# Graph layer on one core: score tables read back by source tile in rows of 2,000 bytes, each piece behind the wait for its own bucket

## What is computed

```python
e = xl[src] + xr[dst]
e = jnp.where(e >= 0, e, NEG_SLOPE * e)
score = jnp.einsum('ehd,hd->eh', e, att)          # 20,000 edges x 4 heads
m = jax.ops.segment_max(score, dst, num_segments=N)
ex = jnp.exp(score - m[dst])
denom = jax.ops.segment_sum(ex, dst, num_segments=N)
alpha = ex / (denom[dst] + SM_EPS)
agg = jax.ops.segment_sum(alpha[:, :, None] * xl[src], dst, num_segments=N)
```

## Time and profile before

| | |
|---|---|
| median of 3 runs | 1064.28 us (1063.62 to 1066.21) |
| profiled execution | 1064.61 us, span 1062.9 us |
| PE busy | 847.4 us (80%) |
| VectorE busy | 779.2 us (73%) |
| ScalarE busy | 352.6 us (33%) |
| POOL busy | 389.4 us (37%), of it the scatters L2314 240.3 us in 184 instructions |
| scatters, first and last start | 113.4 and 482.0 us |
| granted TensorE clock, mean | 0.887 |

### The profile page before, as it was taken

How to read it: one execution, slowest core, us unless ns; L and a number is a source line. 1 busy time by engine, 2 the same in 40 slices (tenths; PEclk the granted TensorE clock), 3 DMA queues, 4 the chain that set the end, 5 groups by cost and what they waited for, 6 DMA issues and landing times.

```text
span 1062.9 us, 18331 instructions
## 1 busy us (share of the span) xinstructions
PE 847.4 (80%) x5485; PEld 737.6 (69%) x5485; DVE 779.2 (73%) x2013; ACT 352.6 (33%) x1004; POOL 389.4 (37%) x321
## 2 busy tenths in 40 slices
PE   4898779895999896803389999758993895899997
PEld 2577667774788885803279999745892684788996
DVE  7778887888766689934778886776879657766636
ACT  0277443452664356602011111002550261221120
POOL 3279365776576656761032221500000000311204
PEclk9998879997999997866579999979896996799999
DMA  8750000002203234210179999730000001788883
GB/s 283 239 169 1 2 2 3 3 3 59 40 4 72 46 80 96 59 21 20 51 253 315 319 325 337 272 130 0 1 2 0 1 2 46 290 292 299 299 334 99
DMA packets 39511, 129.36 MB, mean 122 GB/s; under 512 B 13117, under 2 KB 22411, under 8 KB 31395
## 3 DMA queue, kind: packets, MB, share of 16 engines
q1 hardware_dynamic: 22974, 112.64, 32.0%
q0 software_dynamic: 10464, 8.67, 4.5%
q10 hardware_dynamic: 5992, 7.04, 1.9%
HBM read 108.83 MB, written 19.26 MB: 121 GB/s over the span
## 4 chain that ended last, share of the span: by engine, by line
PE 43%; DMA 18%; POOL 15%; DVE 14%; issue 9%; ACT 1%; POOLq 0%; SPq 0%; DVEq 0%; ACTq 0%
POOL pair_scores L2314 12%; PE bank L880 12%; DMA pair_scores<-arena,pair_cells 12%; PE bank L891 6%; PE bank L600 4%; PE bank L813 4%; DMA arena<-in_exp 2%; POOL arena L2348 2%; PE bank L802 2%; PE bank L668 2%; PE bank L978 2%; PE bank L534 2%; DMA arena<-slot_y,sloti 2%; PE bank L1025 1%; PE bank L524 1%
## 5 line engine op out<-in xcount | busy, mean ns | idle before, releaser
L2314 POOL DMA_INDIRECT pair_scores<-arena,pair_cells x184 | 240.3, 1306 | 137.6 <-DMA pair_scores<-arena,pair_cells 62.7
L2338 POOL DMA_INDIRECT arena<-row_tab,ids x42 | 57.7, 1375 | 440.4 <-DVE ids L1724 433.5
L880 PE MATMUL bank<-arena 128*128 128x128 f32 x1480 | 181.3, 281 | 2.4 <-DMA arena<-in_exp 2.3
L880 PEld LDWEIGHTS bank<-arena 128*128 128x128 f32 x1480 | 175.9, 198 | 4.2 <-DMA arena<-in_exp 3.2
L668 PE MATMUL bank<-x_hi,hot 125*125 x368 | 118.8, 348 | 6.8 <-issue 1.4
L2071 ACT ACTIVATE tc<-bank 125x256 f32<-125x256 f32 x184 | 70.5, 384 | 134.9 <-PE bank L668 126.4
L668 PE MATMUL bank<-x_lo,hot 125*125 x368 | 104.8, 305 | 0.0
L891 PE MATMUL bank<-arena 128*128 128x256 f32 (+1 forms) x404 | 97.5, 384 | 1.3 <-issue 1.3
L668 PEld LDWEIGHTS bank<-x_hi,hot 125*125 125x125 f32 x368 | 76.0, 207 | 20.7 <-issue 18.0
L1302 DVE TENSOR_TENSOR tc<-tc,vec 125x512 f32<-125x512 f32 x92 | 63.8, 693 | 33.9 <-ACT tc L2072 32.4
L802 PE MATMUL bank<-ident,arena 125*125 125x125 f32 x260 | 44.4, 306 | 50.9 <-ACT arena L2121 49.5
(11 more groups left out here) (410 smaller groups left out, 1691.2 us busy)
## 6 DMA issues: line engine op xcount, KB each, us to landing
arena<-in_exp SPq DMA_DIRECT2D x25, 1024.0 KB, 6.6
arena<-in_exp SPq DMA_DIRECT2D x17, 1386.0 KB, 6.2
arena<-in_exp0o SPq DMA_DIRECT2D x25, 512.0 KB, 6.5
pair_scores<-cnt SPq DMA_DIRECT2D x10, 1093.8 KB
arena<-in_exp1o SPq DMA_DIRECT2D x17, 640.0 KB
arena<-pair_scores SPq DMA_DIRECT2D x4, 1093.8 KB
slot_y<-arena ACTq DMA_DIRECT2D x34, 128.0 KB, 6.2
pair_scores<-arena,pair_cells POOLq DMA_INDIRECT x184
```

Source lines behind the costliest of these rows:

```text
L880: mm = pe.matmul(banks[1 + 2 * q + buf][0:rows, i * SLOTS:(i + 1) * SLOTS], w_in(s, q, k, m, rows), xsT[:, s, k, :], start=(k == 0), stop= ...
L2314: p.indirect_dma_start(out=pair_scores[which], in_=sc_ring[:, i, which, :], in_offset=None, out_offset=bass.IndirectOffsetOnAxis(ap=pair_c ...
L2338: p.indirect_dma_start(out=xs[:, q, :], out_offset=None, in_=tab, in_offset=bass.IndirectOffsetOnAxis(ap=ids[:, q, :], axis=0))\
```

## The change

`ENDS` becomes the 24 ends of buckets 0 to 23, so that each bucket but the last has its own. `load_table(m)` becomes a loop over the five source tiles: for each it awaits the scatters up to the end of bucket 5 m + s and loads the piece as tile 4's are loaded, four DMAs in rows of 2,000 bytes. The waits that stood ahead of whole tables go. VectorE's wait for a table counts the semaphores of 20 DMAs in place of 4. Tile 4's pieces are as before, with their ends under new indices; the order of tables, buffers, `h2` and `merged` is unchanged.

```diff
--- before.py
+++ after.py
@@ -80,7 +80,7 @@
 
 BASES = {"before": 0, "rest": EC + 1, "one_of": 0, "cell": BUCKETS * P, "tile": BUCKETS * P + P, "order": BUCKETS * P + P + 3}
 BASES["ends"] = BASES["order"] + BUCKETS
-ENDS = [T * m for m in range(1, T)] + [T * (T - 1) + s for s in range(1, T)]
+ENDS = list(range(1, BUCKETS))
 BASE_SIZES = (2 * (EC + 1), BASES["ends"] + len(ENDS))
 LATE = [(0, (T - 1) * P, tuple(range(T - 1))), ((T - 1) * P, P, (T - 1,))]
 
@@ -1491,7 +1491,7 @@
 
             def table_maxima(m):
 
-                dve.wait_ge(sem(f"sdense{m}"), 2 * 16 * len(PARTS))
+                dve.wait_ge(sem(f"sdense{m}"), T * 2 * 16 * len(PARTS))
                 first, second = (sdense[q] for q in SDENSE[m])
                 v.tensor_tensor(first, first, second, ALU.max).then_inc(sem("merged"), 1)
                 dve.wait_ge(sem("merged"), m + 1)
@@ -2401,14 +2401,12 @@
 
             def load_table(m):
 
-                for w in range(2):
-                    for rows in PARTS:
-                        sp.dma_start(sdense[SDENSE[m][w]][rows, :, :].rearrange("p n h -> p (n h)"), cells[w][m][rows])\
-                            .then_inc(sem(f"sdense{m}"), 16)
-
-            def load_piece(s):
-
-                m = T - 1
+                for s in range(T):
+                    await_scatters(m * T + s)
+                    load_piece(m, s)
+
+            def load_piece(m, s):
+
                 for w in range(2):
                     for rows in PARTS:
                         sp.dma_start(sdense[SDENSE[m][w]][rows, s * P:(s + 1) * P, :].rearrange("p n h -> p (n h)"),
@@ -2416,24 +2414,20 @@
 
             sp.wait_ge(sem("sorting"), SORTING["ends"])
             sp.wait_ge(sem("h2"), 1)
-            await_scatters(0)
             load_table(0)
             sp.wait_ge(sem("h2"), 2)
-            await_scatters(1)
             load_table(1)
             sp.wait_ge(sem("h2"), 3)
-            await_scatters(2)
             load_table(2)
-            await_scatters(3)
             load_table(3)
             sp.wait_ge(sem("merged"), 3)
             for s in range(T - 1):
-                await_scatters(T - 1 + s)
-                load_piece(s)
+                await_scatters(T * (T - 1) + s)
+                load_piece(T - 1, s)
             sp.wait_ge(sem(f"sdense{T - 1}"), (T - 1) * 2 * 16 * len(PARTS))
             for w in range(2):
                 sp.wait_ge(sem(f"scattered{w}"), 16 * PAIRS)
-            load_piece(T - 1)
+            load_piece(T - 1, T - 1)
 
             def expert_weights(name, nblk, nu, w_in, w_outs):
 
```

## The result

The changed kernel takes 1053.49 us in the median of six runs (1046.02 to 1057.98), where the kernel before has 1066.32 in six (1063.62 to 1073.58): a ratio of 0.9867, 95% interval 0.9823 to 0.9911, so 12.8 us off by the medians. Forecast were 1049 in a range from 1036 to 1062, and faster. The profiled execution took 1046.02 us (span 1044.1), 18.6 less than the one of before; it is the fastest of its six, while before's 1064.61 lay 1.7 under its median.

What follows compares the result with a forecast made beforehand. The stream of scatters, held up by table reads, was taken to bound the first attention. Reading tables 0 to 3 in pieces at 0.70 us each would end it 15.5 us earlier: 1064.6 to 1049, range 1036 to 1062.

Steps and rivals of the forecast that it cites:

- The bound: The stream of 184 scatters sets when the first attention ends; a microsecond won there shows in the total.
- The sum: Scatter stream reckoned in blocks past the table reads: last scatter at 466.5 for 482.01, so 15.5 us earlier.
- VectorE's first wait: VectorE's first wait for tile 4's pieces should be gone or small, its second some 12 us.
- The price of the pieces: Each piece read holds the scatters up 0.70 us, between bounds of nothing and 1.95 us.
- the account: A table read's loss to the scatter stream: time over the blocks around it less 1.66 us a block.
- third rival: Each piece has its own price, 1.95 us in SP's burst: 11 us slower, 1076; chance 0.07.
- second rival: Bytes count, not rows: five pieces in a burst hold scatters up like one table; 0.6 us early, 1064; chance 0.11.
- The last: Pieces drain one after another, a table taking 20 us for 10: 32 us slower, 1097; chance 0.02.
- The first rival: Pieces nearly free, VectorE becomes the bound: stream ends 34 us early, gain capped at 27.9 us, 1036.7; chance 0.10.
- Table 3's loss: The whole read of table 3, around blocks 153 and 154, costs the scatter stream 6.4 us.
- scores don't stop the stream: Block 88 needs step 47's reduce, done by 276.15; POOL comes there at about 281.

Runs made afterwards that it cites:

- d4: Changed kernel with tables 0 to 3 not read back (16 bytes a row stand in, results not the program's): 1039.02 us, ratio 0.9760 to the kernel before.
- d2: Changed kernel with tables 0 to 3 in ten pieces each, rows of 992 and 1,008 bytes: 1050.91 us, ratio 0.9864 to the kernel before.
- c2: Changed kernel with one wait a table for tables 0 to 3, so pieces issue without gaps: 1055.73 us, ratio 0.9920 to the kernel before.
- e3: Kernel before with tables 0 to 3 each read in two bursts of 1.22 MB, rows of 10,000 bytes: 1068.90 us, ratio 1.0030.
- c3: Changed kernel with tables 0 to 3 in 10,000-byte rows, DMAs of 16 neighbouring partitions: 1106.39 us, ratio 1.0405 to the kernel before.
- d3: As c3, but each DMA takes every eighth partition: 1057.27 us, ratio 0.9925 to the kernel before.
- e1: Changed kernel with tables 0 to 2 read whole, only table 3 in pieces: 1064.07 us, ratio 0.9991 to the kernel before.
- e2: Changed kernel with table 3 read whole, only tables 0 to 2 in pieces: 1059.16 us, ratio 0.9930 to the kernel before.
- c1: The changed kernel run again, unaltered: 1050.05 us, ratio 0.9879 to the kernel before.
- e4: Changed kernel with table 3's five pieces waiting for buckets 20, 21, 21, 22, 22: 1050.88 us, ratio 0.9862 to the kernel before.

## Why the prediction was right

**The bound.** The stream of scatters set the end and what it won showed in the total: 17.1 us at the last scatter (1.2 of them older than the first read), 18.6 in the profiled executions. By medians 12.8 and 14.7 came of it in two sets. That is 2.7 and 0.8 us less than the 15.5 forecast; the 17.1 and 18.6 are on the high side, since the execution profiled is the shortest of its six. Where single runs differ by 12 us the profile of one can't say which lines make the difference; that stays open. The forecast also took 3.2 us as what a measurement can tell from no change; the first set's interval is wider, 4.7 us to either side.

**The sum.** Its stations, forecast and measured: block 158.9 and 160 at 411; block 166 at 428.2 and 425.52; 173.9 blocks at 447 and block 174 at 448.16; last scatter 463.7 + 2.8 = 466.5 and 464.88. VectorE's first wait was to vanish and did; the second was to be 12 us and was 11.56.

**The price of the pieces.** 0.70 us a piece was taken from two waits of tile 4's pieces; 0.79 was measured by the same account, and 0.47 to 0.49 against d4. As a price of a table in short rows, 3.5 us, it held about (3 to 5 us by the account, for tables 0 and 1, in bursts, apart and in tens); as a price of a piece it is wrong, as d2 shows, and so the third rival falls (a price for each piece, slower from 1.4 us). The second rival (bytes count, not rows) falls with the two tables of c2, where short rows at the rate of a whole table lost about half as much, and with e3, where long rows lost as much in half bursts. Row length and the size of a DMA shrink together wherever the rows are short; small DMAs with long rows were run only in c3 and d3, and d3 leaves a share to pace or size. The last (pieces drain one after another) falls with c2's 258 GB/s: short pieces are neither slow nor in each other's way. With SP's gaps the rate fell from 245 to 199 GB/s, and no wait of VectorE for a table came of it. The Trainium skill ("DMA: Bandwidth & Descriptors", "Bandwidth") asks for transfers of 1 MiB or more. The traces do not agree for DMAs that follow each other: those of 219 and 25 KB moved 258 GB/s in c2, those of 1,094 and 127 KB 245 before. Of the time that rule would have told the wrong sign. The first rival's cap was right as a cap (d4), its condition (a price near nothing) was not met: 9 to 10 us are left in the pieces.

**What was sized wrong.** Table 3's loss before was taken as 6.4 us from one wait; blocks 150 to 156 there took 406.17 to 425.42, 19.25 - 10.0 = 9.3, part of it POOL's slow instructions. From block 78 to 156 the change saved 19.5 us (164.3 to 144.7), more than the 16.2 that the sum's losses and prices give (30.2 less 20 x 0.70). That scores don't stop the stream was held from block 88 alone; in the changed kernel block 144 waited 2.56 us for them. And the sum treated the tables' losses as adding up with the time at the end, which the traces of e1 and e2 speak against.

**A rule of the Trainium skill.** Row first: the longest wait in the read of a whole table was 6.9 to 7.7 us in three tables and 4.0 in one, and in the reads in pieces at most 2.4 (2.8 in c1, 3.4 in e4). The Trainium skill, "DMA: Bandwidth & Descriptors", section "Queues, rings and completion order", says that an engine takes turns between its queues and changes over only at the end of a packet. The traces agree in direction, shorter rows letting the other queue in sooner. They list one transfer for each row: 250 of 10,000 bytes for table 0 before, 633 ns each in the mean, and 1,250 of 2,000 bytes after, 122 ns each. A wait of 7.1 us is as long as eleven of the long ones, so more than one row passed ahead of a scatter; whether several make up one packet of the chip no run shows.

## What to carry to other kernels

Where a stream of small dependent DMAs bounds a stage, look at what bulk reads in flight do to each landing. Cutting a read's rows shorter relieved the stream here most; two half bursts did not, groups of neighbouring partitions made it far worse, and groups of spread partitions issued slowly gave 7.2 us, about half of it. The test is one change of each kind. And work out where the next engine takes over before counting on more: here 28 us, of which short rows gave half.

## What the runs showed of the hardware

- A read of 10,000-byte rows in DMAs of 16 neighbouring partitions ran at 119 GB/s with the engines at a share of 1.00, where 112 and 13 partitions a DMA gave 238 and 16 partitions eight apart 168 at 0.88. It cost 42 us in the total.
- DMAs of 219 and 25 KB in 2,000-byte rows, issued without gaps, moved 258 GB/s (c2), as much as those of 1,094 and 127 KB (245).
- A DMA whose partitions step by eight took SP mostly 0.6 us or more to issue, where one with neighbouring partitions took 0.4 (14.66 us and 9.17 us for the sixteen of table 1, with the register loads between).
- Tables 0 and 1 in 5 or 10 pieces, in a burst or 10 us apart: rows of 2,000 bytes and less cost the stream 3 to 5 us a table by the account, whatever the pieces' number and spacing. We had expected bursts and more pieces to cost more.
- The same program's executions spread over 5 to 15 us in a set (0.5 to 1.4%), the kernel before over 8 to 13, its one execution at 1073.66 aside.
